# A fused layer on eight cores: seven groups in the ternary stage, the fourth pair's chains ahead of a weight transfer, gates after slot 9, scan behind slot 11

## The reference

```
xn  = layernorm(x)                                  # no affine part, eps 1e-5
a   = tanh(xn @ Wa.T + ba);  b = tanh(xn @ Wb.T + bb)     # 64 columns each
h_t = a_t * h_(t-1) + b_t                           # recurrence over the 4096 rows
w   = clip(round(W / (mean|W| + 1e-10)), -1, 1) * mean|W| # W is 2048 x 2048
y   = x + (xn + h @ Wout.T + bout) + (xn @ w.T + bias)
```

## Time and profile before

| | us |
|---|---|
| median of three runs (lowest, highest) | 549.07 (548.84, 550.89) |
| the profiled execution | 545.46 |
| its span on the slowest core, core 3 | 543.9 |
| spans of the eight cores | 535.8 to 543.9 |
| TensorE busy on that core | 467.0 (86%) |
| VectorE busy | 341.8 (63%) |
| ScalarE busy | 215.8 (40%) |
| GpSimd busy | 150.3 (28%) |

### The profile page before, as it was taken

The page is one execution under the profiler, slowest core; times in us unless marked ns, Lnnn a source line. Parts: engine busy times, 40 slices in busy tenths (PEclk is TensorE's granted clock), DMA queues, the critical chain, the costliest instruction groups (busy, mean ns, idle before and its releaser), DMA issues.

```text
span 543.9 us, 8281 instructions; the slowest of 8 cores (535.8 to 543.9 us)
## 1 busy us (share of the span) xinstructions
PE 467.0 (86%) x2323; PEld 223.9 (41%) x2323; DVE 341.8 (63%) x516; ACT 215.8 (40%) x183; POOL 150.3 (28%) x536
## 2 busy tenths in 40 slices
PE   0020489999939999999999999999999999999997
PEld 0010134545424444444444545454545444545443
DVE  2633497969737574857576767666666757573633
ACT  0477395745434334252506070706161615242000
POOL 0400236331634051414233232323241415150000
PEclk9999999999979999999999999999999999999999
DMA  7999980264464948585777667676858584843212
GB/s 225 341 331 344 303 217 1 78 218 112 117 144 152 209 156 219 149 221 156 221 158 213 174 183 205 189 199 174 215 164 224 160 228 155 232 145 88 107 49 116
DMA packets 72048, 99.15 MB, mean 182 GB/s; under 512 B 57090, under 2 KB 57090, under 8 KB 65986
## 3 DMA queue, kind: packets, MB, share of 16 engines
q1 hardware_dynamic: 71328, 97.53, 61.3%
q0 software_dynamic: 384, 1.05, 1.2%
q10 hardware_dynamic: 292, 0.05, 0.1%
HBM read 52.48 MB, written 33.55 MB: 158 GB/s over the span
## 4 chain that ended last, share of the span: by engine, by line
PE 57%; DMA 15%; SPq 10%; issue 4%; POOLq 4%; DVE 4%; ACT 3%; DVEq 2%; POOL 0%; ACTq 0%
PE pu L714 44%; DMA wbuf<-wt 6%; DMA xnT<-wbuf 5%; PE pu L686 5%; PE pab L673 4%; SPq L265 4%; SPq L257 3%; DMA y<-sx 3%; DVE bst L439 2%; ACT wbuf L337 2%; DMA sx<-x 1%; SPq L270 1%; DVEq L441 1%; PE pu L732 1%; PE pu L727 1%
## 5 line engine op out<-in xcount | busy, mean ns | idle before, releaser
L455 DVE SCALAR_TENSOR_TENSOR sx<-pu,scl,sx 128x512 f32<-128x512 f32 x212 | 158.0, 748 | 147.1 <-PE pu L714 80.0
L714 PE MATMUL pu<-wbuf 128*128 128x512 f16 x896 | 204.7, 379 | 0.0
L714 PE MATMUL pu<-wbuf,xnT 128*128 128x512 f16 x672 | 154.2, 379 | 0.0
L714 PEld LDWEIGHTS pu<-wbuf 128*128 128x128 f16 x896 | 87.5, 98 | 103.3
L714 PEld LDWEIGHTS pu<-wbuf,xnT 128*128 128x128 f16 x672 | 65.6, 98 | 79.6
L439 DVE BATCH_NORM_STATS2 bst<-sx 128x6 f32<-128x512 f32 x128 | 78.8, 678 | 14.4 <-DMA sx<-x 14.2
L337 ACT ACTIVATE wbuf<-sx,nmr,yr 128x2048 f16<-128x2048 f32 x26 | 54.3, 2088 | 37.6 <-DMA xnT<-wbuf 31.2
L840 POOL TENSOR_SCALAR uu<-mv 128x1 f32<-128x1 f32 (+1 forms) x29 | 10.1, 348 | 209.5 <-DVE mv L443 201.1
L344 ACT ACTIVATE sx<-sx,nmr,p1r 128x2048 f32<-128x2048 f32 x32 | 66.9, 2093 | 2.4
L686 PE MATMUL pu<-wbuf,xnT 128*128 128x512 f16 x256 | 57.9, 379 | 3.7 <-DVE wbuf L490 2.0
L356 ACT ACTIVATE sa<-pab,bab_s 64x256 f32<-64x256 f32 x16 | 7.5, 468 | 117.8 <-PE pab L673 117.8
(11 more groups left out here) (62 smaller groups left out, 309.6 us busy)
## 6 DMA issues: line engine op xcount, KB each, us to landing
sx<-x SPq DMA_DIRECT2D x32, 1024.0 KB, 6.5
y<-sx SPq DMA_DIRECT2D x63, 512.0 KB, 3.7
wbuf<-wt SPq DMA_DIRECT2D x15, 1024.0 KB, 30.3
wbuf<-wt SPq DMA_DIRECT2D x2, 512.0 KB, 33.5
xnT<-wbuf SPq DMA_TRANSPOSE x52, 3.5
wab_s<-wab POOLq DMA_DIRECT2D x1, 512.0 KB, 12.7
y<-sx SPq DMA_DIRECT2D x2, 256.0 KB, 2.5
wocv<-wo POOLq DMA_DIRECT2D x1, 256.0 KB, 14.6
```

The costliest lines, as they stand in the source:

```text
L455: vector.scalar_tensor_tensor(out, bank(b), scl[:, :], out, OP.mult, OP.add).then_inc(s_ev, 1)
L714: ins = tensor.matmul(bank(b), left(p, lname, c), right(rname, c, h), start=(fresh and c == 0), stop=(state is None and c == HC - 1), skip ...
```

## The change

It leaves the arithmetic as it is and changes orders, one bank and some waits.

- In the ternary stage seven groups are open, not six. The seventh uses the transposes' bank, which `ptr` then shares; the order of the plain units is (1,2), (0,0..3), (1,0), (1,1), (1,3), then tiles 2 and 3 as before, and PE's `turn(2, 0)` waits for the first eviction.
- VectorE rounds five chunks in place of six; chunk 0 is clipped in halves right behind the rounding of each half.
- Statistics of tiles 2, 3, 7 and 6 stand at other places in VectorE's order, some plain evictions too.
- GpSimd: chain(2) and chain(3) apart, and chain(7) and chain(6) ahead of the loads of `wo2`.
- ScalarE: norm(7) ahead of resid(5).
- In the pairs: `gate(n)` behind slot 9, not 7; scan(n) behind `s2(n)`, which stands behind take 11, not behind take 9.

```diff
@@ -36,15 +36,19 @@
 N_AA = len(ABS_ACT) + 2
 N_AD = len(ABS_DVE) + 2
-RND_DVE = [0, 3, 6, 9, 12, 15]
+RND_DVE = [0, 4, 8, 12, 15]
 RND_ACT = [c for c in range(NCH) if c not in RND_DVE]
-PLAIN = [(t, q) for t in range(3) for q in range(NQ)] + [(3, 2), (3, 3), (3, 0), (3, 1)]
+PLAIN = ([(1, 2)] + [(0, q) for q in range(NQ)] + [(1, 0), (1, 1), (1, 3)]
+         + [(2, q) for q in range(NQ)] + [(3, 2), (3, 3), (3, 0), (3, 1)])
 NPL = len(PLAIN)
+NFIRST = 7
+PBANK = [6] + [i % NBANK for i in range(NPL - 1)]
@@ -136,7 +140,7 @@
         two_i = sb("two_i", [128, 2], I32)
         shi = sb("shi", [128, 2], I32)
         pu = e(nc.psum_tensor("pu", [128, NBANK * QW], F32))
-        ptr = e(nc.psum_tensor("ptr", [128, 1024], F16))
+        pt = e(nc.psum_tensor("pt", [128, QW], F32))
         pab = e(nc.psum_tensor("pab", [128, 512], F32))
         s_x = [sem(f"s_x{i}") for i in range(NSX)]
@@ -177,6 +181,9 @@
         s_v = sem("s_v")
         block = e(nc.Block())
+        ptr = pt[:, :].bitcast(F16)
         def wslot(c):
             return wbuf[:, c * D:(c + 1) * D]
@@ -204,6 +211,8 @@
             return xnT[:, (t % 4) * D + lo:(t % 4) * D + hi]
         def bank(b):
+            if b == NBANK:
+                return pt[:, :]
             return pu[:, b * QW:(b + 1) * QW]
         def sfac(n, i):
@@ -316,7 +325,8 @@
             scalar.dma_start(out=xs(5)[64:65, :], in_=bi_d[:, :]).then_inc(s_bi, 16)
             def norm(t):
-                scalar.wait_ge(s_stats, POS[t] + 1 if t >= TURNED else t // 2 * 2 + 2)
+                scalar.wait_ge(s_stats, POS[t] + 1 if t >= TURNED or t in (2, 3) else
+                               t // 2 * 2 + 2)
                 if t == 3:
                     scalar.wait_ge(s_tern, NCH + 1)
@@ -346,7 +356,7 @@
             def evict_T(t, half):
                 scalar.wait_ge(s_tr, 2 * POS[t] + half + 1)
-                scalar.copy(xT(t, half * HD, (half + 1) * HD), ptr[:, :]
+                scalar.copy(xT(t, half * HD, (half + 1) * HD), ptr
                             ).then_inc(s_xnT, 1)
             def gates(n):
@@ -417,14 +427,17 @@
                     resid(a)
                     evict_T(b, 0)
                     evict_T(b, 1)
+                    if n == 2:
+                        norm(7)
                     resid(b)
                 else:
                     norm(a)
                     resid(a)
                 gates(n)
                 states(n)
-                if TURNED // 2 <= n + 1 < NP:
+                if 4 <= n + 1 < NP:
                     norm(b + 2)
+                if 3 <= n + 1 < NP:
                     resid(b + 2)
         @block.vector
@@ -459,7 +472,7 @@
                 t, q = PLAIN[u]
                 vector.wait_ge(s_v, POS[t] + 1)
                 vector.wait_ge(s_unit, u + 1)
-                add_to(xs(t, q * QW, (q + 1) * QW), u % NBANK)
+                add_to(xs(t, q * QW, (q + 1) * QW), PBANK[u])
             def take(p, k):
                 t, lo = target(p, k)
@@ -552,20 +565,18 @@
             vector.drain()
             vector.reciprocal(inv[:, :], scl[:, :]).then_inc(s_inv, 1)
             vector.drain()
-            for lo in (0, HD):
+            for i, lo in enumerate((0, HD)):
                 vector.tensor_scalar(wint[:, lo:lo + HD], wslot(0)[:, lo:lo + HD],
                                      inv[:, :], None, OP.mult).then_inc(s_rnv, 1)
-            for i, lo in enumerate((0, HD)):
-                vector.wait_ge(s_rnv, 2)
+                vector.wait_ge(s_rnv, i + 1)
                 vector.tensor_scalar(wpart(0, lo, lo + HD), wint[:, lo:lo + HD],
                                      -1.0, 1.0, OP.max, OP.min).then_inc(s_tern, 1)
             for c in range(NCH):
                 if c > 0:
                     ternary(c)
-                if c == 3:
+                if c == 5:
                     stats(2)
-                elif c == 6:
+                elif c == 8:
                     stats(3)
                 elif c == 13:
                     scan(0)
@@ -575,29 +586,28 @@
                 if c + 2 in RND_DVE:
                     rounded(c + 2)
-            for u in range(6):
+            for u in range(NFIRST):
                 plain(u)
             stats(4)
             stats(5)
+            plain(7)
             for c in range(0, HC, 2):
                 t1(c)
-            plain(6)
-            plain(7)
             scan(1)
             t3(0)
             t3(2)
             plain(8)
             plain(9)
+            stats(ORD[6])
             t3(4)
             t3(6)
             plain(10)
+            stats(ORD[7])
             plain(11)
-            stats(ORD[6])
-            stats(ORD[7])
             vector.wait_ge(s_T, 8)
             t2(0)
+            t2(2)
             plain(12)
-            t2(2)
             plain(13)
             t2(4)
@@ -630,14 +640,13 @@
                 if m < NP:
                     stats(2 * m)
                 take(p, 8)
-                if n < NP:
-                    scan(n)
                 take(p, 9)
                 if n < NP:
                     s13(n)
                 take(p, 10)
                 if n < NP:
                     s2(n)
+                    scan(n)
                 take(p, 11)
                 if n < NP:
                     s4(n)
@@ -654,6 +663,9 @@
                     tensor.wait_ge(s_xnb, POS[t] + 1)
                 if POS[t] > 0 or half > 0:
                     tensor.wait_ge(s_xnT, 2 * POS[t] + half)
+                if t == 2 and half == 0:
+                    tensor.wait_ge(s_ev, 1)
                 for c in range(8):
                     lo = half * HD + 128 * c
                     ins = tensor.transpose(ptr[:, 128 * c:128 * (c + 1)],
@@ -677,7 +689,7 @@
             def plain_part(u, lo, hi):
                 t, q = PLAIN[u]
-                b = u % NBANK
+                b = PBANK[u]
                 if lo == 0:
                     if b in used:
                         tensor.wait_ge(s_ev, used[b])
@@ -690,7 +702,7 @@
             def plain_mix(u):
                 t, q = PLAIN[u]
                 tensor.wait_ge(s_hsb, t // 2 + 1)
-                tensor.matmul(bank(u % NBANK), hA[:, (t % 4) * TT:(t % 4 + 1) * TT],
+                tensor.matmul(bank(PBANK[u]), hA[:, (t % 4) * TT:(t % 4 + 1) * TT],
                               wocv[:, q * QW:(q + 1) * QW], start=False, stop=True
                               ).then_inc(s_unit, 1)
@@ -771,14 +783,14 @@
             for c in range(NCH):
                 if c == 0:
                     tensor.wait_ge(s_tern, 1)
-                    for u in (0, 1, 4, 5):
+                    for u in (1, 2, 5, 6):
                         plain_part(u, 0, 1)
                     tensor.wait_ge(s_tern, 2)
-                    for u in (2, 3):
+                    for u in (3, 4, 0):
                         plain_part(u, 0, 1)
                 else:
                     tensor.wait_ge(s_tern, c + 2)
-                    for u in range(6):
+                    for u in range(NFIRST):
                         plain_part(u, c, c + 1)
                 if c == 6:
                     tensor.wait_ge(s_wabl, 16)
@@ -786,17 +798,17 @@
             tensor.wait_ge(s_brow, 1)
             tensor.wait_ge(s_hrow, 1)
             tensor.wait_ge(s_wol, 16)
-            for u in range(6):
+            for u in range(NFIRST):
                 plain_mix(u)
             turn(2, 0)
-            plain(6)
+            plain_part(7, 0, HC)
             turn(2, 1)
-            plain_part(7, 0, HC)
-            turn(3, 0)
             plain_part(7, HC, NCH)
             plain_mix(7)
+            turn(3, 0)
+            plain_part(8, 0, HC)
             turn(3, 1)
-            plain_part(8, 0, NCH)
+            plain_part(8, HC, NCH)
             gate(1)
             plain_part(9, 0, NCH)
             plain_mix(8)
@@ -816,7 +828,7 @@
                 n = p + 1
                 for k in range(NSL):
                     slot(p, k)
-                    if n < NP and k == 6:
+                    if n < NP and k == 8:
                         gate(n)
         @block.gpsimd
@@ -868,14 +880,17 @@
                 g.tensor_scalar(hA[64:65, i * TT:(i + 1) * TT], ones[64:65, :],
                                 inv[64:65, :], None, OP.mult)
             g.drain().then_inc(s_hrow, 1)
-            chain(2, 3)
+            chain(2, 2)
+            chain(3, 3)
             chain(4, 5)
+            for t in ORD[TURNED:TURNED + 2]:
+                chain(t, t)
             g.wait_ge(s_unit, 14)
             g.wait_ge(s_T, 8)
             g.dma_start(out=wo2[0:64, :], in_=wo_d[:, HD:D]).then_inc(s_wo2, 16)
             g.dma_start(out=wo2[64:128, :], in_=wo_d[:, HD:D]).then_inc(s_wo2, 16)
-            for t in ORD[TURNED:]:
+            for t in ORD[TURNED + 2:]:
                 chain(t, t)
     return nc
```

## The result

The change makes the kernel slower: 568.84 us median (568.36 to 571.67, four runs) against 548.96 (547.82 to 550.89), a ratio of 1.037 (95% interval 1.032 to 1.041). The forecast was 568. The profiled execution took 568.73 us, its slowest core again core 3.

The account below looks back on a forecast made before the run. Before, the loop through DMA (27.4 us) and TensorE (27.7) were almost level; the moved scan makes the loop bind at 30.5. Fourth-pair turn at 182.5, ten loops and the end give span 563.2, 19.3 more: 549.1 + 19.3 = 568.4 us, range 550 to 580.

Parts of the forecast that it names:

- The loop: From turn(2n) to the next pair's: transposes, load(2m), statistics, scan, states, norm(2m+1), turn(2m+1), store, load(2m+1); 27.4 us before, 30.5 after.
- ten loops of 30.5 us: In the pairs, from the fourth pair's turn at 182.5 us, ten loops through DMA would end at 487.5 us.
- the rival in which the loads shrink: In the pairs, transfers spread over a longer period give a loop of 28.5 us: no change, 549 us; chance 0.07.
- the one in which TensorE stays the bound: In the pairs, the scan's delay is absorbed and TensorE's waits go: faster, 539 us; chance 0.10.
- the one in which every loop is as long as the fourth pair's: In the pairs, all ten loops take 29.6 + 3.1 = 32.7 us: slower still, 590 us; chance 0.06.
- The rule of the Trainium skill: For loads in the pairs, about 2.0 us plus bytes over 436 GB/s; loop 28.5 us, whole 20 us shorter.
- gates at slot 9 ... it isn't what the scan waits for: In the pairs, gates come 3.7 us later, covering most waits, but are done well before the load lands.
- The first stage: Ahead of the pairs, seven groups put TensorE 1.7 us ahead, but later statistics move turn(4, 0) from 117.33 to 119.7 us.
- 2.4 us: Ahead of the pairs, the delay of tiles 4 and 5's statistics, passed on to turn(4, 0); ends 0 to 4 us.
- The third pair: Turn(7) at 143.6, turn(6) at 151.0, gate(3) at 159.3 without a slow gate; the fourth pair begins 5.8 us ahead.
- The waits at gates: From the fourth pair on, each gate finds TensorE waiting some 2.5 to 3 us, since the loop binds.
- The end: Behind the ten loops, last turn at 517.0, last gate at 521.9, span 563.2 us against 543.9.

## Why the prediction was right, point by point

**The loop.** Right in its steps, its price and its cause. The term that carries the sum, ten loops of 30.5 us, measured 30.44 in the mean (29.5 to 31.6). The 3.1 us of instructions ahead of the scan are there without a gap, and the scan put back takes all of the loss away. The landings are what they were (median 6.3 us in both), so the rival in which the loads shrink had nothing to stand on; neither had the one in which TensorE stays the bound (ten gates waited), nor the one in which every loop is as long as the fourth pair's, 32.7. (That TensorE waited before at "five gates of 14" should read of 13; nothing hangs on it.)

**The rule of the Trainium skill** ("DMA: Bandwidth & Descriptors", anatomy of one DMA), by which 4.4 us is the estimate for 1 MB, would have given no change. This trace doesn't agree: no load in the changed kernel's pairs landed under 5.8 us, and the time went by the measured landings.

**Where the scan's delay counts.** The prediction followed one loop. There are two: one over the load and VectorE's queue, one over the gate, slot 8 and take 8. In the changed kernel the first is the longer, so the number held; with the gate behind slot 7 the second is. In the kernel before the gate stood behind slot 7 too, and there the statistics of tile 2m waited for their load in three pairs of 12 only, the fourth among them, by 0.2 to 0.7 us; in the other nine they followed take 8. So in most pairs the load that the prediction put into the loop came to hold it only with the later gates. The step "gates at slot 9 ... it isn't what the scan waits for" was right for the changed kernel, but the step was undervalued: the later gates were taken as a cover for waits, while beside the late scan they save some 15 us (1.065 against 1.037, of 546 us).

**The first stage.** Mixes and turn(4, 0) came when forecast: in the changed kernel's profiled execution the weight's scale was ready 1.6 us later than in the one before (67.81 against 66.20, where VectorE rounds the first chunk), and less that, turn(4, 0) began at 119.8 (119.7 forecast). What failed is the cost behind it: "2.4 us" was 5.3, since the clock fell in the 3.4 us of waiting, and the 17 matmuls and the transposes behind ran 2.9 us over.

```profile
67.81 0.75 DVE L569 TENSOR_SCALAR xnT<-wbuf,inv 128x1024 int16<-128x1024 f32 x1
```

**The third pair.** Two misses that cancel in part: gate(3) came at 162.48, 160.9 with the 1.6 taken off, and not at 159.3. Turn(7) went out at 148.27, and turn(6) at 157.74, 5.1 us later than forecast, 1.6 taken off: 2.9 of it from the clock, the rest since the transposes of turn(7) landed after 7.2 us and not 4.9: they ran beside tile 3's last stores, the last issued 0.6 us ahead of them, and beside load(9); no run tells these two apart. (148.5 and 2.1 are 150.6 and not the 151.0 of the prediction, too.) Behind turn(6) load(9) was all but in, since it landed 1.2 us later, so from turn(6) to the gate it took 4.7 us and not 8.3, and TensorE came just in time. The fourth pair began 3.5 us earlier than before, the 1.6 taken off, and not 5.8.

**The waits at gates** were 2.0 us in the mean and not 2.5 to 3: part of the 2.8 us that a pair loses went into gates at the lower clock and into slots 13 that wait for take 9.

**The end.** Last turn at 519.5, 1.6 off 517.9 (517.0 forecast), span 567.1, 1.6 off 565.5 (563.2 forecast). So the spans of the two profiled executions differ by 23.2 us where 19.3 were forecast. That the median came out within 1 us of 568.4 is in part luck: the forecast counted from a profiled execution 3.6 us under its median, and the changed kernel's lies at its median.

## What to carry to other kernels

Before an instruction is moved back in an engine's order, look at what stands *behind* it on every engine of the chain, not only at what needs its result: here a norm that needs nothing of the scan waited for it, because ScalarE took the states first. When transfers, statistics and queues form a loop from one pair to the next, add up its legs and compare the sum with the bound engine's time per pair; where the two are level, each microsecond put into the loop is paid in every pair, and exchanging two independent instructions can take a leg out.

## What the runs showed of the hardware

The clock of TensorE fell behind waits of 2 to 4 us, but not behind each. In the changed kernel a gate that had waited 3.19 us took 3.57 us, one that had waited 3.33 us took 1.91. TensorE's gates there, and in the kernel before with the scan moved alone:

```profile
255.25 1.91 PE L685 MATMUL pab<-xnT,wab_s 128*128 128x256 f16 x16 [3.33 <-DMA xnT<-wbuf]
315.02 3.57 PE L685 MATMUL pab<-xnT,wab_s 128*128 128x256 f16 x16 [3.19 <-DMA xnT<-wbuf]
```

```profile
289.55 1.91 PE L672 MATMUL pab<-xnT,wab_s 128*128 128x256 f16 x16 [3.99 <-DMA xnT<-wbuf]
379.70 3.56 PE L672 MATMUL pab<-xnT,wab_s 128*128 128x256 f16 x16 [2.34 <-DMA xnT<-wbuf]
```

The granted clock was 0.50 in the gate at 379.70 and 1.00 in the one at 289.55. So the length of the wait alone doesn't tell whether the next gate is slow; a wait of 2.3 us was enough here, and one of 4.0 us wasn't. And a lower clock in a loop that goes through TensorE isn't hidden: with the gates behind slot 7, take 8 began 5.4 us after the slow gate at 290.25, and 3.7 us after the one at full clock at 258.52.

The two transposes of a turn held SyncE's queue for 2.6 us with no load just ahead of them, and for 5.1 to 5.4 us behind load(2m+1) (at 208.51 against 185.90 and 215.95 in the changed kernel). Load(2m) stands behind them in the loop; what that costs, no experiment here shows.
